# First attention: one order of turns, scores, weighing and output over a whole pass instead of one per query tile

## What is computed

```python
q = (hidden_states @ Wq).reshape(b, s, N_HEADS, DN + DR)            # 16 heads, 128 + 64
kv = (_rmsnorm(c, kv_norm_w) @ W_ukv).reshape(b, s, N_HEADS, DN + DV)
scores = jnp.einsum('bqhd,bkhd->bhqk', q_full, k_full) * scale + combined_mask
attn = jax.nn.softmax(scores, axis=-1)
out = jnp.einsum('bhqk,bkhd->bqhd', attn, v).reshape(b, s, N_HEADS * DV)
return out @ Wo
```

## Time and profile before

| what | value |
|---|---|
| time, median of 3 runs | 3084.42 us (3079.48 to 3084.93) |
| profiled execution | 3102.45 us, span of the trace 3100.8 us |
| inner part of attention A in the trace | 753 to 1892 us, four passes |
| second pass | 1046.4 to 1332.9 us |
| busy in the whole span | PE 77%, DVE 66%, ACT 51%, POOL 17% |

### The profile page before, as it was taken

One profiled execution on the slowest core, in us unless ns is written; L12 is line 12 of the kernel. 1 busy time (PEld: TensorE's weight loads), 2 busy tenths in 40 slices (PEclk: granted clock), 3 DMA queues, 4 the chain that ended last, 5 costly groups with the idle time before them and its releaser, 6 DMA issues. The chain is left out here.

```text
span 3100.8 us, 43579 instructions
## 1 busy us (share of the span) xinstructions
PE 2384.1 (77%) x12496; PEld 1567.0 (51%) x12497; DVE 2032.6 (66%) x4228; ACT 1581.9 (51%) x2811; POOL 531.5 (17%) x782
## 2 busy tenths in 40 slices
PE   5935593555999899989989996695439999995882
PEld 2522252225777677767767775353214444434551
DVE  3899689964887688768778875422328877805322
ACT  2776277623665566656556653231206777742230
POOL 0105710571000000000001000313110000000314
PEclk8967896787999999999999997798658999956996
DMA  3011101113000000000000002222270302000223
GB/s 110 1 31 48 61 1 31 48 61 104 22 15 8 23 18 12 11 26 15 11 15 24 9 1 78 69 78 80 92 141 1 42 12 32 1 1 8 82 81 102
DMA packets 83720, 124.30 MB, mean 40 GB/s; under 512 B 26034, under 2 KB 56338, under 8 KB 80530
## 3 DMA queue, kind: packets, MB, share of 16 engines
q1 hardware_dynamic: 70964, 94.04, 11.0%
q0 software_dynamic: 12544, 27.68, 2.8%
HBM read 69.90 MB, written 51.38 MB: 39 GB/s over the span
## 5 line engine op out<-in xcount | busy, mean ns | idle before, releaser
L1145 ACT ACTIVATE aa_pt_hi<-psum 128x512 fp32r<-128x512 f32 x544 | 322.3, 595 | 343.1 <-PE psum L1071 341.5
L1671 DVE TENSOR_REDUCE ab_part_max<-psum 128x2 f32<-128x1024 f32 (+3 forms) x320 | 327.1, 1061 | 119.2 <-PE psum L1509 117.2
L1197 DVE TENSOR_TENSOR aa_pt_lo<-psum,aa_pt_hi 128x512 fp32r<-128x512 f32 x544 | 368.3, 687 | 41.7 <-ACT aa_pt_hi L1145 41.0
L1613 ACT ACTIVATE ab_prob<-psum 128x512 f32<-128x512 f32 (+3 forms) x640 | 298.0, 541 | 120.5 <-PE psum L1538 116.5
L1184 DVE CUSTOM_DVE_ANT_0 aa_prob<-psum,bias 128x512 f32<-128x512 f32 (+2 forms) x480 | 284.4, 597 | 99.9 <-PE psum L1061 93.4
L1059 PE MATMUL psum<-ka_hi,aa_q_hi 128*128 128x512 f32 (+3 forms) x640 | 272.0, 425 | 24.8 <-DVE aa_chunk_max L1184 13.8
L1082 PE MATMUL psum<-aa_pt_hi,c_stack 128*128 128x512 f32 x544 | 257.4, 473 | 41.3 <-DVE aa_pt_lo L1197 40.8
L1071 PE MATMUL psum<-ident,aa_prob 128*128 128x128 f32 x1600 | 266.7, 275 | 5.3 <-issue 4.0
L1040 POOL TENSOR_TENSOR aa_q_lo<-aa_q_row,aa_q_hi 128x512 fp32r<-128x512 f32 x64 | 85.3, 1333 | 1069.7 <-ACT aa_q_hi L1129 1069.7
L1538 PE MATMUL psum<-ab_q_stack,ab_k_stack 50*128 50x512 f32 (+3 forms) x640 | 242.6, 459 | 13.8 <-ACT ab_prob L1613 8.9
L594 PE MATMUL psum<-ixt_w_heads,xT 128*128 128x512 f32 x256 | 154.9, 739 | 124.6 <-ACT ixt_q_nat L547 90.7
(11 more groups left out here) (343 smaller groups left out, 4784.5 us busy)
## 6 DMA issues: line engine op xcount, KB each, us to landing
q_rows<-ixt_q_out SPq DMA_DIRECT2D x64, 256.0 KB, 2.0
aa_q_row<-q_rows SPq DMA_DIRECT2D x64, 256.0 KB, 2.6
f_rows_in<-sent SPq DMA_DIRECT2D x80, 128.0 KB, 2.0
done<-f_rows_out POOLq DMA_DIRECT2D x80, 128.0 KB, 2.0
w<-in_w SPq DMA_DIRECT2D x6, 896.0 KB, 7.3
sent<-ixp_zeros SPq DMA_DIRECT2D x4, 1280.0 KB, 10.4
x<-in_hidden SPq DMA_DIRECT2D x2, 2048.0 KB, 11.1
ab_q_stack<-stash_q_hi SPq DMA_DIRECT2D x32, 128.0 KB, 10.5
```

The costliest lines, as they stand in the source:

```text
L1145: nc.scalar.activation(pt_hi[(TB[t] + j) % RING][:], turn_bank[(TB[t] + j) % RING], ACT.Copy).then_inc(pt_hi_done, 1)
L1197: nc.vector.tensor_tensor(pt_lo[ring][:], turn_bank[(TB[t] + j) % RING], pt_hi[ring][:].bitcast(F32), ALU.subtract).then_inc(pt_lo_done, 1)
L1613: nc.scalar.activation(prob[i % 2][h][:, 0:w], t_bank[slot % RING][:, 0:w], ACT.Exp).then_inc(t_taken, 1)
L1671: nc.vector.tensor_reduce(part_max[e % 2][:, at:at + 5:4, part], s_pair[pair % 2][:, :, 0:w], AX.X, ALU.max).then_inc(s_used, 1)
```

## The change

`plan` is replaced by `events`, one list for a whole pass, with time counted in turns from the pass's beginning (`TB[t]` is the number of turns ahead of tile t). Within a tile turns and scores keep their relative times. A weighing always stands three turns behind its turn, so that those of a tile's last three blocks fall behind turns 0, 1 and 2 of the next tile. `keep` becomes an entry of the list, right behind the tile's last weighing, and so does `invert`, at 0.9 turns into its tile. The output of a tile stands 1.1 and 2.1 turns behind its last weighing, that is 3.1 and 4.1 turns into the next tile; for small tiles this reaches into the tile after. `total` and `inv` get four buffers instead of two. The exponentials keep their lag of 4 entries but come no later than the first turn that needs them. The output of tile 15 still ends the pass, and turns and scores of the next pass come behind it, as before.

```diff
-LAG, SPLIT_AT, SCORES_BY, Y_AT = 3, 0.4, 0.75, (0.1, 0.3)
+LAG, SPLIT_AT, SCORES_BY, Y_AT, INVERT_AT = 3, 0.4, 0.75, (1.1, 2.1), 0.9
...
+    SUMS = 4
...
-        total = [sb(f"total{p}", [P, GH]) for p in range(2)]
-        inv = [sb(f"inv{p}", [P, GH]) for p in range(2)]
+        total = [sb(f"total{p}", [P, GH]) for p in range(SUMS)]
+        inv = [sb(f"inv{p}", [P, GH]) for p in range(SUMS)]
...
-        def plan(t, left, scored, split):
...
+        def events(last):
             todo = []
-            for j in range(t + 1):
-                todo.append((j / (t + 1), ("turn", j)))
-                todo.append(((j + LAG) / (t + 1) + 2e-6, ("weigh", j)))
-            if left:
-                todo += [(Y_AT[pair], ("y", pair)) for pair in range(GH // 2)]
-            if scored:
-                n = GH * chunks[(t + 1) % NT]
-                for k in range(n):
-                    todo.append(((k + 0.5) / n * SCORES_BY, ("score", *divmod(k, chunks[(t + 1) % NT]))))
-            if split:
-                todo.append((SPLIT_AT, ("split",)))
+            for t in range(NT):
+                for j in range(t + 1):
+                    todo.append((TB[t] + j, ("turn", t, j)))
+                    todo.append((TB[t] + j + LAG + 2e-6, ("weigh", t, j)))
+                end = TB[t] + t + LAG
+                todo.append((end + 3e-6, ("keep", t)))
+                todo.append((TB[t] + INVERT_AT, ("invert", t)))
+                todo += [(end + Y_AT[pair] if t < NT - 1 else TN + NT, ("y", t, pair)) for pair in range(GH // 2)]
+                if not last or t + 1 < NT:
+                    n = GH * chunks[(t + 1) % NT]
+                    for k in range(n):
+                        todo.append((TB[t] + (k + 0.5) / n * SCORES_BY * (t + 1),
+                                     ("score", t + 1, *divmod(k, chunks[(t + 1) % NT]))))
+                if not last or t + 2 < NT:
+                    todo.append((TB[t] + SPLIT_AT * (t + 1), ("split", t + 2)))
             return [what for _, what in sorted(todo, key=lambda one: one[0])]
 
         def behind(steps, lags):
 
-            mine = [(n + lags[what[0]], n, what) for n, what in enumerate(steps) if what[0] in lags]
+            begun = {what[1]: n for n, what in enumerate(steps) if what[0] == "turn" and what[2] == 0}
+            mine = [(min(n + lags[what[0]], begun.get(what[1], len(steps)) - 0.5) if what[0] == "score" else n + lags[what[0]],
+                     n, what) for n, what in enumerate(steps) if what[0] in lags]
             return [what for _, _, what in sorted(mine)]
...
             before()
             with eng.Fori(0, NG - 1) as i:
-                passes(i, False)
-            passes(NG - 1, True)
+                run(i, events(False))
+            run(NG - 1, events(True))
...
-                step(i, t, ahead, steps):
-                    for what in behind(steps, {"split": 0, "score": 4, "turn": 0}):
+                def run(i, steps):
+                    for what in behind(steps, {"split": 0, "score": 4, "turn": 0, "keep": 0}):
...
-                    keep(i, t)
...
                     dve.wait_ge(exp_done, g * GH + GH)
-                    dve.wait_ge(x_added, (g - 1) * GH + 4 * GH)
+                    dve.wait_ge(x_added, (g + 1) * GH)
...
-                def step(i, t, ahead, steps):
-                    invert(i, t)
-                    for what in behind(steps, {"score": 0, "turn": 3, "y": 1}):
+                def run(i, steps):
+                    for what in behind(steps, {"score": 0, "turn": 3, "invert": 0, "y": 1}):
...
```

More of the change, by code:

```diff
@@ L1006, in behind, with at, walk @@
             return [what for _, _, what in sorted(mine)]
-        def walk(eng, before, step, finish):
-            def passes(i, last):
-                for t in range(NT):
-                    ahead = [(i + (t + n) // NT, (t + n) % NT) for n in (1, 2)]
-                    there = [not last or t + n < NT for n in (1, 2)]
-                    step(i, t, ahead, plan(t, t > 0, *there))
-                finish(i)
+        def at(i, t):
+            return i + t // NT, t % NT
+        def walk(eng, before, run):
@@ L1105, in before @@
                         score(0, 0, h, 0)
-                def step(i, t, ahead, steps):
+                def run(i, steps):
                     for what in steps:
                         if what[0] == "score":
-                            score(*ahead[0], *what[1:])
+                            score(*at(i, what[1]), *what[2:])
                         elif what[0] == "turn":
-                            turn(i, t, what[1])
+                            turn(i, *what[1:])
                         elif what[0] == "weigh":
-                            weigh(i, t, what[1])
+                            weigh(i, *what[1:])
                         elif what[0] == "y":
-                            leave(i, t - 1, what[1])
-                def finish(i):
-                    for pair in range(GH // 2):
-                        leave(i, NT - 1, pair)
-                walk(pe, before, step, finish)
+                            leave(i, *what[1:])
+                walk(pe, before, run)
             @block.scalar
@@ L1222, in before @@
                     dve.sem_inc(pt_lo_done, RING)
-                    dve.sem_inc(inv_done, 2)
+                    dve.sem_inc(inv_done, SUMS)
                     dve.sem_inc(x_added, 4 * GH)
@@ L1231, in before, with run @@
                         take(0, 0, h, 0)
-                def step(i, t, ahead, steps):
-                    invert(i, t)
-                    for what in behind(steps, {"score": 0, "turn": 3, "y": 1}):
+                def run(i, steps):
+                    for what in behind(steps, {"score": 0, "turn": 3, "invert": 0, "y": 1}):
                         if what[0] == "score":
-                            take(*ahead[0], *what[1:])
+                            take(*at(i, what[1]), *what[2:])
                         elif what[0] == "turn":
-                            split_turned(i, t, what[1])
-                        else:
-                            add(i, t - 1, what[1])
-                def finish(i):
-                    for pair in range(GH // 2):
-                        add(i, NT - 1, pair)
-                walk(dve, before, step, finish)
+                            split_turned(i, *what[1:])
+                        elif what[0] == "invert":
+                            invert(i, what[1])
+                        else:
+                            add(i, *what[1:])
+                walk(dve, before, run)
 def prepare_b(nc, arg, xT, bank, stash, values):
```

23 lines of the change are left out of this document (12 added, 11 removed).

## The result

The change made the kernel slower: 3107.97 us median against 3083.42 of the kernel before in runs on the same chips, a ratio of 1.0076 (95% interval 1.0063 to 1.0089). The forecast was 3072 us, so the sign was wrong, and the time lies above the range.

The account below looks back on a forecast made before the run. The prediction took PE as the engine to follow, waiting for DVE's low half and takes. Its tile groups summed to -3.5 us a pass, -14 for four, clock +2: -12 on 3084.4, 3072 us, range 3046 to 3096.

Parts of the forecast that it names:

- The chain of tile 1: Tile 1 loses two pairs of adds, a DVE wait and some border, gains `invert`: -2.5 us, near 7.3 instead of 9.9.
- tiles 10 to 14: Borders shorten and weighings fill nearly all score waits: -1.1 us per tile, -5.5 for five, bounds -2.5 and -7.
- the price of `invert`: On DVE, `invert` moves from idle time to between first and second take: 0.45 us more per tile.
- Tiles 5 to 9: DVE, the later engine, is held up by +0.9 us per tile, 4.5 for five.
- tiles 3 and 4: As the five tiles after them, but some adds move into the border: +0.45 us each, 0.9 for two.
- if all of them go, PE pays +0.6 per tile: Tiles 3 to 9: PE's border cost of +1.4 us, less score waits of 0.76 if the weighings fill them all.
- rival 2: Heads keep their score waits because DVE starts later as PE does; weighings fill nothing; 3088 us, chance 0.22.
- Tile 15: First weighing needs the previous tile's `keep`; ACT's copy of some 0.6 us is not covered: +0.4, bounds 0 and +0.6.
- Tiles 0 to 2: No engine is full; shorter chains from adds and waits that leave: -3.8 us a pass, bounds -2 and -5.
- The clock: PE's clock falls to half behind some bare border waits, 2.4 falls instead of 1: +1.7, rounded to +2 us.
- rival 3: Bare waits at 12 borders a pass let the clock fall at every second one: +29 us, 3098 us, chance 0.08.
- Rival 4: Border waits vanish because the last exponential ends before PE is there; about half of 86.5 us gone: 3040 us, chance 0.10.

Follow-up runs that it names:

- e2: Changed kernel with `invert` put back ahead of DVE's first take; stage 1154.9 us against 1166.3, ratio 1.0017 to the kernel before.
- e1: Changed kernel with exponentials that stood ahead of `keep` on ACT moved right behind it; stage 1153.0 us against 1166.3, ratio 1.0043 to the kernel before.
- e7: Changed kernel with `keep` ahead of the exponential and `invert` ahead of the first take; stage 1144.3 us against 1166.3, ratio 1.0020 to the kernel before.
- e4: Changed kernel with the next tile's scores given out over the first 0.60 of a tile's turns, not 0.75; stage 1140.3 us, ratio 0.9969 to the kernel before.
- e3: Changed kernel with weighings and `keep` back ahead of the next tile's first turn, outputs still late; stage 1165.4 us, ratio 1.0083 to the kernel before.

## Why the prediction was wrong

**What held.** The places: the turns directly behind the last exponential, PE idle ahead of them (0.4 to 1.7 us by the brackets, in tiles 4 to 15; forecast 1.3 to 1.9), the weighings' waits for DVE gone (86.5 to 4.8 us), the end of the pass in its old order. The chain of tile 1: 7.5 us, forecast 7.3. Tile 12: 24.7, forecast 24.6; tiles 10 to 14 gave -4.7 a pass, forecast -5.5. And the price of `invert` in tiles 5 to 9: 0.44 a tile by e2, 0.45 in the sum, though tile 9 paid nothing and tile 6 0.7, so that the agreement of the mean is partly luck.

**What failed**, by the terms of the sum, 10.5 us a pass between forecast (-3.5) and result (+7.0):

1. *Tiles 5 to 9, +9.2 instead of +4.5 (tile 8 took 20.8 us, forecast 18.8); tiles 3 and 4, +2.7 instead of +0.9.* Two things. `keep` behind an exponential on ACT was missing from the sum: 3.3 us a pass by e1 (2.2 in tiles 5 to 9, 0.8 in tile 4; the other 0.3 lies in tiles 0 to 2 and 15, where the clock differs between the two traces as well). The prediction priced `keep` only in tile 15, by its own length of 0.6 us; it looked at what the copy costs and not at what stands ahead of it in ACT's queue. 

   The second is the price of the weighings themselves. The sum took the later of two engines: DVE, held up by 0.46 without `invert`, against PE with "if all of them go, PE pays +0.6 per tile". They didn't go. The waits of the scores, second pass, tiles 3 to 9, then tiles 10 to 14:

```profile
PEld psum L1060 <- DVE aa_chunk_max L1182: 4.8, 13, 1.0
```

```profile
PEld psum L1060 <- DVE aa_chunk_max L1182: 1.5, 5, 0.5
```

Before they were 5.3 and 4.0. In the long tiles the weighings did fill most of the score waits; in the short ones they filled nearly nothing, as if DVE had begun later by as much as PE. Two things differ there: the turn of a long tile comes 1 us or more sooner than before, and DVE is busy for 20.34 of 25.7 us in tile 12 but for 15.04 of 17.9 in tile 8. Which of them counts more was not isolated. With `keep` and `invert` mended (e7) 0.96 us a tile is left of the 1.4 that three weighings cost, where the forecast without `invert` had 0.46. This is rival 2's mechanism, but in tiles 3 to 9 alone; prediction and rival each took one answer for all tiles, and each kind of tile had its own. The allowance for tiles 3 and 4 (half, because of the adds) had no ground either: they paid 0.94 on the mean in e7, as much as the others.

2. *Tile 15, +2.6 instead of +0.4.* The sum counted weighings across 12 borders and forgot that tile 15's head takes the last three of tile 14 too: 3 x 0.46 = 1.4 us, and tile 15 has no scores of a next tile whose waits they could fill. `keep(14)` cost 0.69 (0.45 in the bracket, which counts from the end of the turn's bar; by the starts, `weigh(15,0)` stands 1.05 us behind `turn(15,3)` where the next one needs 0.36), and the second output, which waited for the adds, the rest, some 0.5. No exponential stands ahead of `keep(14)`, and e1 left this wait as it is. The copy and the weighing:

```profile
1323.97 0.59 ACT L1149 ACTIVATE aa_out_t<-psum 128x512 f32<-128x512 f32 x1
...
1324.71 0.47 PE L1083 MATMUL psum<-aa_pt_hi,c_stack 128*128 128x512 f32 x1 [0.45 <-ACT aa_out_t L1149]
```

3. *Tiles 0 to 2, -2.8 instead of -3.8*, and *tiles 10 to 14, -4.7 instead of -5.5.* Sizes, within their bounds. Tile 2 ran partly at half clock in the second and the fourth pass, 10.1 and 10.4 us instead of 8.8, which is 0.7 on the mean: without it the group stands at -3.5. The 0.45 that the sum had for `invert` in tile 2 didn't show: at full clock tile 2 takes 8.8 us with `invert` in either place (passes 1 and 3 of both traces).

4. *The clock.* Its term (+2 us) and rival 3 rested on a fall behind every tenth or so bare wait. Ahead of the first turns of tiles 4 to 14 not one fall came. The stage spent 43.9 us at half clock before and 57.6 after, nearly all at its start, about the ends of the passes and in tiles 1 and 2; that is 13.7 us more, four stretches of 3.4, and by the price of the earlier trace rows (1.2 us for one) an estimated 5 us for the whole stage, already contained in the tiles' lengths above. The term was too small by some 3 us, and its place was wrong. It also means that a difference of some 5 us between two stages is within what the clock can do.

Why the range missed too: its upper bound allowed +7 for tiles 3 to 9 together, and the three missing prices (3.3 for `keep`, 2.5 to 3.5 for score waits not filled, 2.2 in tile 15) all add on one side. Its ends were not formed alike either: the lower one, 3046, holds the clock's +2, the upper one, 3096, doesn't; with it, 3098, it would have missed all the same. Rival 4 had named the right lever, the last exponential, but as something that the change would do by itself; it took the earlier scores of e4.

**What stays open.** With both mends, a short tile pays 0.96 us, between the +0.6 of waits filled and the 1.3 that the score waits (5.3 to 4.8) would leave; where the difference of 0.35 to the latter comes back was not isolated. Nor was it shown why tiles 3 to 9 and tiles 10 to 14 answer differently. The gain of tiles 0 to 2 was not split into its steps, because e3 brought a wait of its own there.

## What to carry to other kernels

A wait that other work fills costs nothing until that work moves. Before moving it, ask what it will fill in its new place, and whether the border that they leave gets shorter: three weighings moved out of a covered wait cost 0.96 us a tile where the last exponential set the turn anyway (tiles 3 to 9), and paid where the turn had waited for them (tiles 10 to 14). And a step that moves on one engine has a successor on another: look up what stands ahead of it in that queue, since a copy of 0.6 us behind an exponential of 1.36 held PE for 1 us in three tiles of every pass, 13.3 us in all. Finally, test an order together with what it makes possible: earlier scores cost 23 us in the old order and gave 26 in the new one.

## What the runs showed of the hardware

Bare waits between long tiles hardly lowered TensorE's clock. In the changed kernel PE stood idle ahead of a first turn 61 times, 81.1 us in all. About the waits of 0.4 to 1.7 us ahead of the first turns of tiles 4 to 14, 44 of them, the granted clock stayed at 1.00 (2.4 GHz). The falls to half (1.2 GHz) came at the ends of the first and second pass (13.7 us each from 1050.7 and 1344.3), at the end of the third and, for 3.4 us, in tiles 1 and 2 of the second and the fourth, as here in the second:

```profile
1060.98 0.68 PE L1072 MATMUL psum<-ident,xT 128*128 128x128 f32 x2 [1.94 <-ACT aa_prob L1134]
...
1068.43 1.11 PE L1072 MATMUL psum<-ident,aa_prob 128*128 128x128 f32 x4 [2.61 <-ACT aa_prob L1134]
```

There the turn of four matmuls takes 1.11 us, against 0.60 at full clock, behind a wait of 2.61. The window about it has a clock of 0.72, with the end of the longer stretch before it:

```profile
1062.10:1072.10 10.00, 7.39 (x29) 5.98 (x29) 5.56 (x18) 5.62 (x13) 1.28 (x1) 0.72 0.09 29
```

Tiles 1 and 2 differ from the later ones in more than this one wait, and what lets the clock fall there was not tried. The third pass shows that the wait alone does not decide: in it PE waits 2.77 us ahead of tile 2, and the clock stays full.

Harmless is not the same as never. The kernel before has the one fall behind a wait between long tiles that the prediction counted, at the border of tile 13 in the third pass:

```profile
1565.07 0.71 PE L1082 MATMUL psum<-aa_pt_hi,c_stack 128*128 128x512 f32 x1 [1.62 <-DVE aa_pt_lo L1197]
...
1566.01 1.06 PE L1071 MATMUL psum<-ident,aa_prob 128*128 128x128 f32 x4
```

The same wait in its other three passes brought none. In the traces of the other twelve kernels the clock never fell in tiles 4 to 14. The Trainium skill, "TensorE: Matmul & The Clock Gate", section "HAM oscillation — how this bites in real kernels", tells of a kernel in which a wait for a DMA behind each short stretch of matmuls put the clock back to half, so that every following stretch started slow. The prediction stretched that to each of these 48 shorter waits. At the borders of tiles 4 to 14 the traces show one such fall, in the kernel before, and none in the changed kernel; in the first tiles of a pass they show it in two passes of four.
